# Random-feature attention stage: the second normalisation placed behind the additions of norms, its input held twice, the value products in another bank, and GpSimd's last parts in later slots

## The reference

```
x1 = x + layernorm(attn(layernorm(x)))
q, k, v = split(h @ w_qkv.T)              # 16 heads of 8
f(t)    = exp(t @ rf.T / 8 - |t|)         # 64 features a head
kv      = f(k).T @ v ;  norm = f(q) @ sum_n f(k)
attn    = ((f(q) @ kv) / (norm + 1e-6)) @ w_out.T + b_out
```

## Time and profile before

| | before |
|---|---|
| median of 3 runs | 1735.05 us (1734.45 to 1735.18) |
| profiled execution | 1734.0 us |
| its span | 1731.8 us |
| busy PE / DVE / ACT / POOL | 94% / 86% / 75% / 67% |
| stage A, from the start to the first load of stage T | 0 to 349.7 us |
| granted TensorE clock | 0.992 of full speed |

### The profile page before, as it was taken

One profiled execution on the slowest core, in us unless ns is written; L12 is line 12 of the kernel. 1 busy time (PEld: TensorE's weight loads), 2 busy tenths in 40 slices (PEclk: granted clock), 3 DMA queues, 4 the chain that ended last, 5 costly groups with the idle time before them and its releaser, 6 DMA issues. The chain is left out here.

```text
span 1731.8 us, 53966 instructions
## 1 busy us (share of the span) xinstructions
PE 1625.4 (94%) x17733; PEld 1106.6 (64%) x17861; DVE 1487.6 (86%) x3284; ACT 1298.7 (75%) x3588; POOL 1155.8 (67%) x1143
## 2 busy tenths in 40 slices
PE   5888888869999999999989998999999999998997
PEld 3555555537777676777766655777777777775664
DVE  4899999878998998999868767998999999996996
ACT  5888888848998999899872225999899899985221
POOL 2666666677777777777753225777777777775664
PEclk9999999999999999999999999999999999999999
DMA  3211111111111111111123321111111111113443
GB/s 117 72 50 48 48 51 49 48 43 44 43 38 40 43 33 42 45 33 42 42 61 95 95 67 30 47 34 42 45 33 42 43 35 42 40 37 86 115 123 85
DMA packets 201098, 94.04 MB, mean 54 GB/s; under 512 B 82579, under 2 KB 192061, under 8 KB 201021
## 3 DMA queue, kind: packets, MB, share of 16 engines
q1 hardware_dynamic: 201020, 93.06, 20.3%
HBM read 51.00 MB, written 25.23 MB: 44 GB/s over the span
## 5 line engine op out<-in xcount | busy, mean ns | idle before, releaser
L878 ACT ACTIVATE pr<-banks,nb,rr 128x128 f32<-128x128 f32 x1024 | 455.5, 464 | 5.6 <-DVE nb L947 5.6
L779 POOL TENSOR_TENSOR rr<-ss,half_neg 128x16 f32<-128x16 f32 x128 | 374.3, 2924 | 19.0 <-POOL ss L776 17.1
L796 POOL TENSOR_TENSOR pr<-pr,rl 128x512 f32<-128x512 f32 x256 | 266.0, 1040 | 101.8 <-DVE rl L909 101.8
L917 DVE TENSOR_REDUCE ss<-sq 128x16 f32<-128x1024 f32 x128 | 156.2, 1220 | 80.6 <-ACT sq L827 66.9
L1248 ACT ACTIVATE f_g<-banks,b_s 128x512 f32<-128x512 f32 (+1 forms) x96 | 65.8, 686 | 200.9 <-PE banks L1332 192.7
L878 ACT ACTIVATION_READ_ACCUMULATOR pr<-banks,nb,rr 128x1 f32 x1024 | 216.1, 211 | 0.0
L925 DVE TENSOR_REDUCE mx<-banks 128x8 f32<-128x1024 f32 x128 | 156.0, 1219 | 9.2 <-PE banks L1054 8.4
L787 POOL TENSOR_TENSOR krot<-ka,rr 128x512 f32<-128x512 f32 x128 | 134.9, 1054 | 22.3 <-POOL rr L779 11.6
L869 ACT COPY pT<-banks 128x512 f32<-128x512 f32 x128 | 75.1, 586 | 96.1 <-PE banks L1006 96.1
L1006 PE MATMUL banks<-ident,pr 128*128 128x128 f32 x1024 | 140.7, 280 | 5.9 <-POOL pr L796 5.9
L1054 PE MATMUL banks<-kT,qT 64*64 64x128 f32 x2048 | 140.6, 277 | 0.0
(11 more groups left out here) (125 smaller groups left out, 4241.6 us busy)
## 6 DMA issues: line engine op xcount, KB each, us to landing
ve<-vt SPq DMA_DIRECT2D x128, 128.0 KB, 2.2
hs<-y_d SPq DMA_DIRECT2D x128, 64.0 KB, 1.9
yt<-y_d SPq DMA_DIRECT2D x64, 128.0 KB, 2.1
y_d<-yn SPq DMA_DIRECT2D x64, 128.0 KB, 2.0
f_h<-y_d SPq DMA_DIRECT2D x128, 64.0 KB, 2.0
f_y<-y_d SPq DMA_DIRECT2D x64, 128.0 KB, 2.2
xa<-in_L_attn_x SPq DMA_DIRECT2D x32, 128.0 KB, 2.1
xr<-in_L_attn_x SPq DMA_DIRECT2D x32, 128.0 KB, 2.3
```

The source lines that it names most:

```text
L779: nc.gpsimd.tensor_tensor(rr[:, r, :], ss[:, r, :], half_neg[:], ALU.pow).then_inc(T["rr"], 1)
L796: nc.gpsimd.tensor_tensor(pr[:, e], pr[:, e], rl[:, e].unsqueeze(2).broadcast_to([P, UH, P]), ALU.mult).then_inc(T[("ne", "no")[e]], 1)
L878: a = nc.scalar.activation(pr[:, e, j, :], bank[e][:, j * P:(j + 1) * P], ACT.Exp, bias=nb[:, X.t, UH * e + j:UH * e + j + 1], scale=rr[:, ...
L917: nc.vector.tensor_reduce(ss[:, 2 * X.p + X.t, :], sq[:].rearrange("p (h d) -> p h d", d=DH), AX.X, ALU.add).then_inc(T["ss"], 1)
```

## The change

There are four edits.

1. `a_y` gets two halves by the parity of the batch. On DVE the second normalisation of batch i - 3 moves from ahead of the bias addition to behind the additions of norms (L658).
2. The wait of the bias addition for `yn` goes back by one batch.
3. The values are written to the lower half of bank 6, in which `a_xn` is turned, and no longer to the upper half of bank 7. PE's L572 no longer waits for `y`; it waits for `xT` and `v`, and L610 waits for `v` in addition.
4. POOL's part 2 of the end of stage A is cut into parts 2 (inverse standard deviation) and 3 (L483). For step B + 1 part 3 goes from ahead of slot 2 to ahead of slot 3; for step B + 2 parts 2 and 3 go from ahead of slot 3 to ahead of slots 5 and 6, and SP's last stores of stage A go from ahead of slot 5 to ahead of slot 7.

```
-        a_y = sa("a_y", [P, TPB, D])
+        a_y = sa("a_y", [P, 2, TPB, D])
...
-            if on.last and part in (None, 2):
+            if on.last and part in (None, 3):
                 pool.wait_ge(A["rs3"], n + 1)
...
-                                       bank[7][:, N + t * P:N + (t + 1) * P].rearrange("p (j e) -> p j e", e=16))
+                                       bank[6][:, N + t * P:N + (t + 1) * P].rearrange("p (j e) -> p j e", e=16))
...
             if on.now:
-                if on.tail:
-                    pe.wait_ge(A["y"], k + 1)
+                if on.ahead:
+                    pe.wait_ge(A["xT"], i + 2)
+                until(pe, A["v"], i)
                 for t in range(TPB):
-                    m = nc.tensor.matmul(bank[7][:, N + t * P:N + (t + 1) * P], a_xT[:, p, t * P:(t + 1) * P],
+                    m = nc.tensor.matmul(bank[6][:, N + t * P:N + (t + 1) * P], a_xT[:, p, t * P:(t + 1) * P],
                                          wT[:, 2, :], start=True, stop=True)
...
-            if on.last and part in (None, 1):
-                dve.wait_ge(A["rs2"], l + 1)
-                until(dve, A["x1"], l)
-                for t in range(TPB):
-                    j = normal(a_y2, a_y, a_mv2, a_rs2, t)
-                j.then_inc(A["yn"], 1)
             if on.tail and part in (None, 1):
                 dve.wait_ge(A["w_ps"], k + 1)
                 if on.last:
-                    dve.wait_ge(A["yn"], l + 1)
-                nc.vector.tensor_tensor(a_y[:], bank[7][:, 0:N].rearrange("p (t d) -> p t d", d=D),
+                    until(dve, A["yn"], l)
+                nc.vector.tensor_tensor(a_y[:, p], bank[7][:, 0:N].rearrange("p (t d) -> p t d", d=D),
...
+            if on.last and part in (None, 1):
+                dve.wait_ge(A["rs2"], l + 1)
+                until(dve, A["x1"], l)
+                for t in range(TPB):
+                    j = normal(a_y2, a_y[:, 1 - p], a_mv2, a_rs2, t)
+                j.then_inc(A["yn"], 1)
             if on.next:
                 dve.wait_ge(A["rs"], i + 3)
...
-                if k == 5:
+                if k == 7:
                     a_sync(sp, B + 2, A2, odd=False)
...
-                if k in (1, 2):
+                if k in (1, 2, 3):
                     a_pool(pool, B + 1, A1, odd=True, part=k)
-                if k in (2, 3):
-                    a_pool(pool, B + 2, A2, odd=False, part=k - 1)
+                if k in (2, 5, 6):
+                    a_pool(pool, B + 2, A2, odd=False, part=(2, 5, 6).index(k) + 1)
```

More of the change, by code:

```diff
@@ L594, in a_pe @@
                 pe.wait_ge(A["qf"], 2 * n + 2)
-                if on.now:
-                    pe.wait_ge(A["v"], i + 1)
                 if on.tail:
@@ L608, in a_pe @@
                 until(pe, A["xT"], i + 2)
+                until(pe, A["v"], i + 1)
                 for t in range(TPB):
@@ L672, in a_dve @@
                 until(dve, A["rs2"], k)
-                stats(dve, a_y, a_st2, a_mv2, TPB, A["st2"], 2 * (k + 1), A["mv2"])
+                stats(dve, a_y[:, p], a_st2, a_mv2, TPB, A["st2"], 2 * (k + 1), A["mv2"])
             if on.last and part in (None, 2):
```

## The result

| | before | changed |
|---|---|---|
| median of 5 runs | 1735.05 us (1733.87 to 1735.57) | 1727.4 us (1722.89 to 1729.26) |
| ratio, with its 95% interval | | 0.9953 (0.9936 to 0.997) |
| profiled execution, its span | 1734.0, 1731.8 us | 1729.26, 1727.4 us |
| last L658 (L652) of stage A begins | 340.64 us | 331.23 us |
| first turn of `hs` on PE | 352.30 us | 344.61 us |

The change made the kernel faster by 7.65 us. The forecast was a tie at 1734.8 us, in a range of 1728.0 to 1742.5. The changed kernel lies just outside that range, and beyond the 1731.6 us that the forecast named as the bound for a tie.

What follows compares the result with a forecast made beforehand. DVE's serial chain was taken to bound stage A's 10.41 us step. Stage A -0.45 and seam +0.2 gave -0.25 us on 1734.0, so 1733.75; plus 1.05 for the runs' median, 1734.8 us, range 1728.0 to 1742.5.

Steps and rivals of the forecast that it cites:

- a tie: Whole kernel: time within a few us of before, likeliest case 1730 to 1738.5 us, chance 0.66.
- the neighbour comes back: Stage A's step: POOL's L465 now lands on DVE's first normalisation and delays it, a loss of 0.47 us a step.
- The rival without collision: Stage A's step: L465 does not disturb the first normalisation; step 9.91 us, time 1723.0 us, chance 0.12.
- L634: DVE in stage A's loop: starts 1.2 to 1.3 us behind L625, waiting for PE; gain 0.42 us a step.
- The pair of L652: DVE in stage A's loop: L465 no longer runs beside this pair; it takes 1.4 us, a gain of 0.60.
- the pair in its new place: DVE's second normalisation behind the additions of norms: takes 0.6 us with POOL idle, a loss of 0.52 a step.
- Taking the pair out of cover in step 3: Stage A's step 3: the second normalisation leaves a wait that stays, costing 0.3 to 0.4 us once.
- The exclusive lock for L483: POOL's L483 beside DVE's additions of norms: costed at nothing; as slower rival +7.8 us, 1742.6 us, chance 0.11.
- Values in bank 6: PE's values in stage A: L572 no longer waits for `y`, but cost and gain are 0.
- The seam: Passage from stage A to stage T: later load and moved POOL parts sum to +0.2 us.
- The later load: Seam: stage T's first load comes 1.6 us later, since `x1` hangs on the moved normalisation; +1.5 us.
- POOL's last parts: Stage T's early slots: less work ahead of slot 3 gives -1.2 and -0.3 us, slot 6 costs +0.2.

Runs made afterwards that it cites:

- after_unrolled: The changed kernel with stage A written out in full instead of a hardware loop: 1735.18 us, ratio 1.0014 to the kernel before.
- before_hs_first: The kernel before, with SP's load of `xr` of step 32 put behind stage T's first load: 1733.45 us, ratio 1.0003.
- bank_only: The kernel before with only the values moved to bank 6, PE's waits changing with it: 1735.11 us, ratio 0.9994.
- after_hs_first: The changed kernel, with SP's load of `xr` of step 32 put behind stage T's first load: 1724.18 us, ratio 0.9936 to the kernel before.

## Why the prediction was wrong

**What failed: the term "the neighbour comes back", +0.47 us a step.** The prediction let L465 start 0.08 us behind the end of the pair, from the earlier trace rows. Those rows are of step 32, outside the loop. In the loop of the kernel before, no row shows this delay: there L465 stood behind L483, which ended at 216.63 with L465 at 216.60. In the loop of the changed kernel the delay is 0.29 to 0.34 us, the second instruction of the first normalisation gets in, and the term is 0. The prediction saw that L465 could be later in the loop, and drew the wrong sign from it: it priced a later start dearer ("some 0.5"), with a row in which POOL was first by 0.02 us. The case that came, both instructions in front of L465, it named as a rival and gave a chance of 0.12. Outside the loop the term was right: 0.41 us at 53 us (1.01 less 0.60), and 0.42 a step in the unrolled kernel (10.24 less 9.82). With stage A unrolled the forecast of a tie would have held (1735.18 us), in part by luck: the step there was 10.24 us and not the 10.38 of the forecast, and more was lost behind the last L652 than it had.

**Point by point, the rest of the step was right.** L634 came 1.32 us behind L625 (219.30, 220.62), waiting for PE, forecast 1.25. The pair of L652 took 1.41, forecast 1.42; the pair in its new place 0.60. The rival without collision gave 9.91 us for the step, and 9.94 came. Taking the pair out of cover in step 3, forecast 0.3 to 0.4, cost 0.33 (10.12 against 9.79 us).

**The exclusive lock for L483** cost nothing in the loop. The overlap of 0.53 us came as worked out (L483 ends at 212.20, L652 begins at 211.67), and L652 took its plain time. Written out, it did cost something. In the changed kernel's loop the second L483 begins at 211.40 and L652 0.27 us behind it; in after_unrolled it is 0.12 (before rounding):

```profile
226.56 0.80 POOL L478 TENSOR_SCALAR a_yo<-a_x,a_mv,a_rs 128x128 f32<-128x128 f32 x1
226.69 0.87 DVE L647 SCALAR_TENSOR_TENSOR xn<-nrm,hones,qkm 128x512 f32<-128x512 f32 x1
```

The first instruction of the pair took 0.87 us instead of 0.75. This repeats across the traces: an L652 that began less than 0.23 us behind the start of an L483 ended 0.98 to 0.99 behind that start (97 instructions), and one that began 0.24 or more behind it took its plain 0.75. So L483 held it up over its own first 0.24 us and not to its end. Nothing here shows why. The forecast had this term at nothing, which was right in the loop and some 0.12 us a step short in the written-out kernel.

The Trainium skill, SBUF — State Buffer, section "Who interferes with whom", gives the pair of ports that DVE and GpSimd share to whoever issues first, for the whole instruction, where DVE's instruction is in a 2-port mode, which `tensor_scalar` (L406) can enter, or reads two inputs in SBUF while GpSimd's reads SBUF too. For L465 the trace agrees: the L406 that came second ended 0.09 us behind it (228.65 + 1.01 = 229.66 against 228.82 + 0.76 = 229.58). By the same section of the Trainium skill a DVE instruction with at most one SBUF input outside the 2-port modes does not contend. The statistics beside L465 agree (0.47 us for the pair). For L483 beside L652 the measurement differs, and it decides. The prediction counted L1230 to the case of two inputs as well; its neighbour L406 reads one tensor, and belongs to that of the 2-port mode.

**Values in bank 6 at nothing:** right.

**The seam, +0.2 us: wrong in two parts.** The later load, +1.5, was right in size (1.72 to PE's first turn). POOL's last parts, -1.5 together, were not: the wait of DVE's statistics for `yo`, with L917 behind it, was left out, and it made slot 3 0.87 us later instead of sooner. The clock was in no term. In all, what lies behind the last L652 lost 1.1 us in one execution and 4.1 in another; how much of that is the clock is not settled.

**The sum of the measured:** with the same first periods, stage A ends 10.3 to 10.7 us sooner (341.48 and 341.88 in before_hs_first and bank_only, 331.23). The period behind the first L652 scatters from 9.56 to 11.62 us over the traces, whatever the kernel. In the profiled execution of the kernel before it was 10.12 and in the changed one 11.27, which is why these two show a lead of only 9.41. With 1.1 to 4.1 us lost behind the last L652 this makes 6 to 10 us, and the measured 7.65 lies between. The forecast also left the time around the span alone; it was 2.15 us in the kernel before and 1.84 in the changed one, and no run shows why.

## What to carry to other kernels

When two engines contend for a few tenths of a us, ask who begins first in each shape of the code, and take the delay from a semaphore to the next engine's start from that same shape: looped steps carry register instructions that written-out steps don't. When a step is moved on one engine, look up every wait for its semaphore on the others, and what is queued behind that wait. And look for short waits of an engine for its own last instruction: here the second normalisation, put into such a wait of 0.23 us and beside statistics that L465 does not disturb, was worth about as much again as the whole change (0.9937 to 0.989, and 1 to 0.9953).

## What the runs showed of the hardware

- A 128x2 memset on POOL (0.23 us) did not hold up the 128x256 addition behind it: that began 0.07 us behind the memset's start. With a wait on its semaphore it began 0.33 behind it.
- A lead of about 0.07 us by the trace is no lead. In the five traces with the old order L658 began 0.067 to 0.077 us ahead of L465 in 125 steps. In 94 of them L658 paid (1.34 us instead of 0.75), among these all 65 with 0.071 or less; in the other 31 L465 paid (1.26 instead of 0.72).
- An L406 on 128x128 that began 0.1 us behind POOL's L465 took 0.75 us instead of 0.34. When both L406 were ahead, they took 0.34 each, and L465 0.80 instead of 0.73.
- An L652 that began less than 0.23 us behind the start of an L483 on POOL ended 0.98 to 0.99 us behind that start; one that began 0.24 or more behind it was not held up.
- The granted clock of TensorE fell to half behind a wait of PE of 2.73 us, in one execution for the whole stretch of 7 us, in another, with a wait of 2.68, for half of it. Where PE did not wait (after_hs_first) it fell too, 5.8 us behind PE's first turn. The first L1071 at half clock took 2.08 us for its two products, 1.12 at full.
- In a loop of two steps a round the periods alternated between 9.84 and 10.04 us; written out, with L465 held back, most were 9.82.
